# Hybrid attention, selective scan and mixture-of-experts on one core: the sum over the scan's 16 states moves from GpSimd's additions into TensorE's accumulation

## What is computed

```python
def selective_scan(u, delta, A, B, C, D):
    dA = jnp.einsum('bld,dn->bldn', delta, A)
    dB_u = jnp.einsum('bld,bld,bln->bldn', delta, u, B)
    dA_shift = jnp.concatenate([dA[:, 1:], jnp.zeros_like(dA[:, :1])], axis=1)
    dA_cumsum = jnp.exp(jnp.flip(jnp.cumsum(jnp.flip(dA_shift, axis=1), axis=1), axis=1))
    xs = jnp.cumsum(dB_u * dA_cumsum, axis=1) / (dA_cumsum + 1e-12)
    y = jnp.einsum('bldn,bln->bld', xs, C)
    return y + u * D
...
y = selective_scan(x, delta, A, B, C, D)
return jnp.einsum('bld,de->ble', y, W_out) + b_out
```

## Time and profile before

| | us |
|---|---|
| median of 3 runs | 1469.24 (1466.34 to 1470.05) |
| the profiled execution | 1482.02 |
| its span | 1480.3 |
| PE busy | 1006.6 |
| DVE busy | 827.8 |
| ACT busy | 745.5 |
| POOL busy | 633.3 |
| mean granted TensorE clock | 0.788 of 2.4 GHz |

### The profile page before, as it was taken

The page is one execution under the profiler, slowest core; times in us unless marked ns, Lnnn a source line. Parts: engine busy times, 40 slices in busy tenths (PEclk is TensorE's granted clock), DMA queues, the critical chain, the costliest instruction groups (busy, mean ns, idle before and its releaser), DMA issues.

```text
span 1480.3 us, 18066 instructions
## 1 busy us (share of the span) xinstructions
PE 1006.6 (68%) x5080; PEld 742.0 (50%) x5080; DVE 827.8 (56%) x2789; ACT 745.5 (50%) x2034; POOL 633.3 (43%) x672
## 2 busy tenths in 40 slices
PE   4778588757787755588697863678688647871371
PEld 2555377625666433457476622366476316650371
DVE  3677655655565775655566673745656754662111
ACT  4777676646555755545566652352454443450020
POOL 2100400173342537560424268785455686456304
PEclk8565589858797857788888956789889867995696
DMA  9000424222322011334434221254444223523472
GB/s 267 4 1 0 127 93 148 79 85 88 103 88 84 13 33 58 121 96 138 132 105 139 79 81 32 84 160 157 128 150 164 84 63 118 160 83 101 129 220 73
DMA packets 101812, 150.65 MB, mean 102 GB/s; under 512 B 9840, under 2 KB 72688, under 8 KB 101584
## 3 DMA queue, kind: packets, MB, share of 16 engines
q1 hardware_dynamic: 88832, 129.20, 27.9%
q0 software_dynamic: 8528, 18.19, 4.3%
q10 hardware_dynamic: 4352, 2.10, 0.5%
HBM read 125.39 MB, written 28.25 MB: 104 GB/s over the span
## 4 chain that ended last, share of the span: by engine, by line
PE 36%; DVE 20%; ACT 16%; POOL 12%; issue 10%; DMA 4%; another core or an unknown queue 2%; SPq 1%; POOLq 0%; DVEq 0%; ACTq 0%
PE eo_bank L1300 9%; PE h_bank L1285 8%; ACT sc_bank L644 7%; PE sc_bank L1234 6%; DVE Pw L892 4%; POOL xg L564 3%; POOL rings L508 3%; DVE rings L902 3%; DVE nmx L836 3%; PE mix_bank L1157 2%; PE sc_bank L1178 2%; POOL gbuf L577 2%; ACT rings L689 2%; DVE eos L1024 2%
## 5 line engine op out<-in xcount | busy, mean ns | idle before, releaser
L1300 PE MATMUL eo_bank<-wring,hid 128*128 128x128 f32 x1472 | 222.0, 300 | 84.9 <-DVE eos L1024 81.5
L644 ACT ACTIVATE sc_bank<-sc_bank,nmx 128x256 f32<-128x256 f32 x512 | 229.8, 457 | 45.7 <-DVE nmx L836 41.4
L1300 PEld LDWEIGHTS eo_bank<-wring,hid 128*128 128x128 f32 x1472 | 202.5, 213 | 96.2 <-ACT hid L718 51.7
L1285 PE MATMUL h_bank<-xT,wring 128*128 128x128 f32 x1472 | 226.6, 302 | 34.6 <-DVE xT L1012 22.0
L1285 PEld LDWEIGHTS h_bank<-xT,wring 128*128 128x128 f32 x1472 | 204.7, 212 | 70.5 <-issue 33.7
L718 ACT ACTIVATE hid<-h_bank 128x512 f32<-128x512 f32 x184 | 109.2, 594 | 230.2 <-PE h_bank L1285 215.3
L508 POOL TENSOR_TENSOR rings<-Rs,Abc 128x512 f32<-128x512 f32 x128 | 163.0, 1288 | 138.9 <-ACT Rs L672 83.1
L1234 PE MATMUL sc_bank<-Pw,upto 128*128 128x512 f32 x256 | 165.7, 747 | 57.9 <-DVE Pw L892 57.2
L836 DVE TENSOR_REDUCE nmx<-sc_bank 128x2 f32<-128x512 f32 x256 | 169.8, 684 | 58.1 <-PE sc_bank L1178 47.5
L577 POOL DMA_INDIRECT gbuf<-yg,pos x128 | 122.9, 960 | 168.2 <-issue 102.0
L902 DVE SCALAR_TENSOR_TENSOR rings<-sc_bank,bc,rings 128x128 f32<-128x128 f32 x512 | 143.0, 342 | 74.5 <-PE sc_bank L1234 74.2
(11 more groups left out here) (155 smaller groups left out, 1364.5 us busy)
## 6 DMA issues: line engine op xcount, KB each, us to landing
wring<-wcat SPq DMA_DIRECT2D x184, 512.0 KB
stage<-xg SPq DMA_DIRECT2D x40, 256.0 KB, 5.0
yg<-eos SPq DMA_DIRECT2D x40, 256.0 KB
wcat<-in_w SPq DMA_DIRECT2D x16, 256.0 KB, 5.2
X<-in_x SPq DMA_DIRECT2D x16, 128.0 KB, 5.1
xg<-xnb,pos POOLq DMA_INDIRECT x128
gbuf<-yg,pos POOLq DMA_INDIRECT x128
out<-X ACTq DMA_DIRECT2D x16, 128.0 KB
```

The costliest lines, as they stand in the source:

```text
L644: last = act.activation(sc[r % NSC][:, c * L:(c + 1) * L], sc[r % NSC][:, c * L:(c + 1) * L], ACT.Exp, bias=nmx[:, c, r:r + 1], accum_out= ...
L1285: last = pe.matmul(hb[b % 2][:, f], wring[:, n % WR, 0, f], xT[:, b % 2], start=True, stop=True)
L1300: last = pe.matmul(eo[:, o:o + P], hid[:, b % 2, f], wring[:, n % WR, 1, f], start=(k == 0), stop=(k == FC - 1))
```

## The change

The weighted blocks are no longer added by POOL. `scan_yT` now has four parts; a part takes two chunks, that is 8 blocks of 128 x 128, each as the stationary operand of a product with the identity, all accumulating in one region of `mp`. So sum and transpose are one. The skip term is a ninth product in parts 1 and 3. All 8 chunks have a record slot, so ACT's waits for the additions are gone; the first chunk's L waits for the last y of the sequence before. In stages with a head, the parts stand in halves 5 to 8, and all that follows y in them (ACT's copy, projection, norm, logits, routing) stands three halves later (`ST_LATE`); in the others the parts stand in halves 1, 2, 4 and 5 and nothing is shifted.

```diff
-        SLOTS, REC_SLOTS = 4, 6
+        SLOTS, REC_SLOTS = 4, CHUNKS
...
-        ysum = sb("ysum", [P, 4 * D])
-        y_s = sb("y_s", [P, T, P])
...
+        ST_LATE = 3
+        Y_PARTS = {True: (5, 6, 7, 8), False: (1, 2, 4, 5)}
...
-            def scan_sum(b, k):
-
-                c = k // 4
-                pool.wait_ge(*scan_dve.at(f"X{k}", b))
...
-                pool.tensor_tensor(ysum[:], ysum[:], rec_slot(k), ALU.add).then_inc(*scan_pool.done(f"add{k}"))
...
             def scan_rest(b):
 
                 pool.wait_ge(*scan_dve.at("u", b))
-                wait_latest(pool, (scan_pool, "yD", b - 1))
+                wait_latest(pool, (scan_pe, "yT", b - 1))
...
-            def scan_skip(b):
-                pool.wait_ge(*scan_pool.at("y1", b))
-                pool.tensor_tensor(y_s[:], y_s[:], uD[:], ALU.add).then_inc(*scan_pool.done("yD"))
...
             def scan_L(b, k):
 
                 act.wait_ge(*scan_act.at(f"E{k}", b))
-
-                if k >= REC_SLOTS:
-                    last = k - REC_SLOTS
-                    act.wait_ge(*scan_pool.at(f"add{last + (last % 4 == 0)}", b))
-                elif k == 0:
-                    wait_latest(act, (scan_pool, "y1", b - 1))
+                if k == 0:
+                    wait_latest(act, (scan_pe, "yT", b - 1))
...
-            def scan_yT(n, b):
-                if n in head:
-                    pe.wait_ge(*attn_dve.at(f"qk{HG - 1}", head[n]))
-                else:
-                    mp_free(n)
-                pe.wait_ge(*scan_pool.at("yD", b))
-                transposes(mp, y_s, scan_pe, "yT")
+            def scan_yT(n, b, part):
+
+                if part == 0:
+                    if n in head:
+                        pe.wait_ge(*attn_dve.at(f"qk{HG - 1}", head[n]))
+                    else:
+                        mp_free(n)
+                c, k = part // 2, 2 * part + 1
+                pe.wait_ge(*scan_dve.at(f"X{k}", b))
+                y = mp[:, c * P:(c + 1) * P]
+                for i in range(8):
+                    last = pe.matmul(y, rec_slot(k - 1 + i // 4)[:, i % 4 * D:(i % 4 + 1) * D], ident[:],
+                                     start=(part % 2 == 0 and i == 0), stop=False)
+                if part % 2 == 1:
+                    pe.wait_ge(*scan_pool.at("uD", b))
+                    last = pe.matmul(y, uD[:, c], ident[:], start=False, stop=True)
+                if part == 3:
+                    last.then_inc(*scan_pe.done("yT"))
...
-                    if half == 5 and ct is not None:
-                        scan_yT(n, ct)
-                    if half == 6 and ct is not None:
+                    if ct is not None and half in Y_PARTS[a is not None]:
+                        scan_yT(n, ct, Y_PARTS[a is not None].index(half))
+                    if half == 6 + s and ct is not None:
                         scan_proj(ct)
```

More of the change, by code:

```diff
@@ L743, in phase @@
                         attn_oT(at)
-                    if half == 5 and ct is not None:
+                    if half == 5 + s and ct is not None:
                         scan_yT(ct)
@@ L753, in phase @@
                         scan_softplus(c)
-                    if half == 7 and ct is not None:
+                    if half == 7 + s and ct is not None:
                         rstd(prep_act[2], prep_dve[2], ct, p_mv, p_lv, p_rs)
@@ L757, in phase @@
                         rstd(attn_act, attn_dve, head[n + 1], a_mv, a_lv, a_rs)
-                    if half == 8 and ct is not None:
+                    if half == 8 + s and ct is not None:
                         prep_xnT(2, ct)
@@ L763, in phase @@
                         route_exp(1, at // GS)
-                    if half == 11 and ct is not None and ct % GS == GS - 1:
+                    if half == 11 + s and ct is not None and ct % GS == GS - 1:
                         route_exp(2, ct // GS)
@@ L1070, in phase @@
                         route_hot(1, at // GS)
-                    if half == 9 and ct is not None:
+                    if half == 9 + s and ct is not None:
                         prep_top(2, ct)
@@ L1318, in phase @@
                 o = AT_LATE if a is not None else 0
+                s = ST_LATE if a is not None else 0
                 for half in range(HALVES):
```

53 lines of the change are left out of this document (10 added, 43 removed).

## The result

The changed kernel takes **1489.47 us** (median of 4 runs, 1482.32 to 1490.18) where the kernel before takes 1467.95 (4 runs, 1466.34 to 1470.05). The ratio is 1.0135, with an interval of 1.010 to 1.017: slower by 21.5 us. Beside the experiments it was measured again, at 1.0126 (1.0086 to 1.0166).

A forecast was written before the change was run, and what follows sets the result against it. No engine was full; PE bound stages with an expert run, POOL was busiest in 24 and 29. Terms -11.4 - 14.3 + 32.9 + 7.3 + 33.3 = +47.8 us gave 1517 us, own range 1495 to 1545, 8 in 10: 1472 to 1556.

The forecast's parts named there:

- +33.3: Products in stages 25, 26, 27, 28, 30, 31: 6 x 7.3 = +43.8 us, less what covers them, together +33.3.
- The additions' 5.7 us come back in each: -11.4 us: Stages 24 and 29: POOL is 7.9 us late; removing the tail's additions gains 5.7 us in each.
- PE waited for `y_s` 18.9 us in 4 times [...]; no gain is counted: PE's waits for `y_s`: the parts of y take its place, so no gain from 18.9 us.
- The products' price: PE's new products: 0.2225 us each, 7.3 us a sequence, 117 us in all; 73.5 us of products counted in the sum.
- The slope of 0.9 us of time for each us of PE: Stages 10 and 18 against 14 gave 0.88 and 0.95 us of time per us of PE; 0.9 taken.
- The 10.5 us of cover: Token waits in stages 27 and 30 (-3.6), POOL's 4.3 us lateness in 25, run ends in 28 and 31 (-2.6).
- ACT's waits, -14.3 us: ACT's waits for additions before L6: -3.8 us in stage 9, -3.5 in 29, -3 in 24, -2 in 17, -2 all others.
- Rival 1: PE's idle time takes the products in, only POOL's gains stay: 1443.5 us; chance 0.17.
- Rival 2: Denser PE work raises the clock in stages 14, 16, 24 and 29, worth -14 us: 1503; chance 0.08.
- Rival 3: Products of every stage but 24, 29 and 32 lie on the path at 10.0 us: +104, 1573; chance 0.12.
- Rival 4: Half or two thirds of the 73.5 us of products hides: +11 or -1, 1468 to 1480; chance 0.08.
- What would show it: Signs: POOL about 460 us busy, PE about 1140, stages 18 and 27 longer by 6 to 8, 24 and 29 shorter.

The follow-up runs named there:

- kernel 2: The kernel before with eight record slots instead of six, so ACT's L6 and L7 wait for no addition; 1462.48 us, ratio 0.9957.
- kernel 8: The kernel before with eight slots, with PE summing y for sequences 7 and 12 only and POOL for the other fourteen; 1436.51 us, ratio 0.9778.
- kernel 3: The kernel before with only the shift by three halves in stages with a head; 1467.68 us, ratio 1.0.
- kernel 1: The changed kernel without its 32 block products a sequence, only the skip term left in y; 1404.34 us, ratio 0.9569.
- kernel 4: The shifted kernel before, POOL still adding, with 34 more products of constants a sequence at the places of the parts; 1529.11 us, ratio 1.042.
- kernel 10: The version with sequences 7 and 12 on PE, with POOL also adding for them into an unread `y_s`; 1459.66 us, ratio 0.9949.
- kernel 5: The changed kernel with each block product made a second time against zeros, y unchanged; 1593.36 us, ratio 1.0841.
- kernel 9: The version with sequences 7 and 12 on PE, without the block products of these two; 1433.89 us, ratio 0.9777.
- kernel 6: The changed kernel with parts 0 and 1 of y moved behind S7 in stages without a head; 1509.37 us, ratio 1.0279.

## Why the effect was under half of the forecast, and what was right

The effect came out as follows, each step against the one before it: eight slots -7 us (kernel 2); sequences 7 and 12 on PE -26 (kernel 8 against 2); the other fourteen on PE +51 (the changed kernel against 8, 1487.4 to 1436.5). The sum is +18 by these and +21.5 by the first pair of medians.

By place, from the traces (us; stages 31 and 32 go from the `u_s` of stage 31 to the first transpose of the last run). The products' cost is once taken with the additions there (kernel 3 to 4) and once without them (kernel 1 to the changed one), the removal's worth once with the products (kernel 4 to the changed one) and once without (kernel 3 to 1):

| stages | products: forecast | with additions | without | removal: forecast | with products | without |
|---|---|---|---|---|---|---|
| 10 to 22, even | +40.2 | +43.9 | +44.4 | part of -2 | -6.0 | -6.5 |
| 24 and 29 | 0 | +0.1 | 0.0 | -17.9 | -25.8 | -25.7 |
| 25 to 28, 30 to 32 | +33.3 | +23.0 | +43.9 | part of -2, and 4.3 in the +33.3 | -7.2 | -28.1 |

- **The step that failed: "The additions' 5.7 us come back in each: -11.4 us", and with it "PE waited for `y_s` 18.9 us in 4 times [...]; no gain is counted".** What taking the additions away is worth was priced too low, at 25.7 us where it is 40 to 63. In stages 24 and 29 it gave 26 us, not 11.4 (and not 17.9 with ACT's waits). The price was read from R's side: POOL is 7.9 us late, so no more than that can be gained, and 5.7 us is the work that goes. Both bounds were wrong. The 7.9 us was what was left of POOL's lateness *after* R had itself been held 4 to 5 us by PE's wait for `y_s`; with that wait gone it is 12 (kernel 10). And the work that goes is not the tail's share alone: the main share stands in the same list ahead of the scatters, and its waits for X2 and X3 went too. Kernels 8 and 10 show it: 36 to 38 us from exponents to exponents with the additions in the list, 24 to 26 without.
- **The same error in stages 25 to 32, where the larger part of the missing 26 us lies.** The sum gave them +33.3; from kernel 3 to the changed one it is +15.8, which is +43.9 for the products and -28.1 for the removal. The forecast knew 4.3 us of POOL's lateness in stage 25 and none in stage 30, again read behind an R that was itself late in that trace (`uT` to R 14.9 us, for 10.3 to 11.3 in both stages of kernels 2, 3 and 8). Three places of the removal's worth are seen in the traces. They are the 7 and 4 us by which POOL is late in stages 25 and 30 (below), and PE's wait for `y_s` in stage 32, 5.4 us of the 18.9.
- **The products' price was right.** Forecast 73.5 us in all; measured 61 with the additions there and 85 without them (the square above). In stages 25 to 32 it is 43.9 without them, beside the 43.8 from which the forecast took 10.5 for waits. A product took 0.235 us in a dense stretch and 0.25 in the mean, where 0.2225 was taken. The slope of 0.9 us of time for each us of PE is 0.92 for the second set of products (kernel 5: 104 us of time for 113 us of PE), but 0.56 from kernel 3 to 4 (61 for 110). Free in 24 and 29 was right (kernel 9).
- **What covers the products was wrong.** The 10.5 us of cover in stages 25 to 31 (the run's tokens, POOL's lateness in 25, the end of the runs) don't show in the changed kernel. "Nothing behind them can take them in" is wrong where the additions stay: there the products cost 23.0 us. And "two parts stand ahead of S6 and S7 [...], so all lie upstream of R" is wrong for these two in stages 24 and 29: they fill waits of PE there (kernel 6). From the trace before to the changed kernel's the stages with a run and no head grew by 0.3 (stage 25), 0.7 (26), 5.3 (27), 3.9 (28) and 2.9 us (30), which is products less removal.
- **ACT's waits, -14.3 us:** 7 (kernel 2). Stage 9 gave its 3.8; stages 24 and 29 gave 1.2 and 2.1 for 3 and 3.5, with POOL's list as long as before (36.4 and 37.7 us in the table).
- **The shift, 0:** right in sum (kernel 3).
- **Stages with a head and a run, 10, 12, 18, 20, 22:** +3.9, +5.4, +2.3, +4.9 and +12.8 against a forecast of 6.6 each, +29.5 for +32.9 in sum. That 18 has so little and 22 nearly twice its share is in good part the shift's doing: kernel 3 alone has -5.1 and +4.4 there, and the block products by themselves (kernel 1 to the changed one) add 8.8 and 6.7. **Stage 14, half of 7.3:** +3.0.
- **Rival 1** (the products hide): falls by kernels 4 and 5. **Rival 2** (the clock pays): the granted clock of stages 24 and 29 did go from 0.63 to 0.77 and 0.81, and both shrank by far more than 9 us; in stage 29 that is the very sign that the forecast had named. It is not the cause. Kernel 9 has the same short stages at 0.69 and 0.70, and kernel 10 has long ones (62 and 57 us) at a clock of 0.70 as well. The Trainium skill ("TensorE: Matmul & The Clock Gate", the clock gate) says that activity releases the throttle; the trace agrees that the denser stages have the higher clock, but these stages were bound by POOL. The sign was badly chosen, since a POOL that comes free gives it too. **Rival 3:** falls; the groups stood at 0.94 us for four products in the dense stretches, and the time is 84 us below its 1573. **Rival 4** (half or two thirds hidden, 1468 to 1480) is 9.5 us away at its upper end, nearer than the forecast's 1517. Its reason holds only where the additions stay; in the changed kernel the products cost more than forecast, not half.
- **What would show it:** POOL 462 of a forecast 460, ACT's waits gone, first exponents close behind R: right. PE 1100, 94 more for a forecast of 120 to 160; stages 18 and 27 longer by 2.3 and 5.3 (6 to 8 forecast), 24 and 29 shorter by 12.7 and 14.2 (6 to 9 forecast): wrong.

**POOL's lateness in stages 25 and 30.** In kernel 3 R's copy on ACT ends at 956.23 us in stage 25, and POOL's first exponents begin 9.0 us later:

```profile
955.85 0.38 ACT L673 ACTIVATE Rs<-mix_bank 128x256 f32<-128x256 f32 x1
```

```profile
965.28 1.27 POOL L509 TENSOR_TENSOR rings<-Rs,Abc 128x512 f32<-128x512 f32 x1
```

| us | stage 25: `uT` to R | R to first exponents | stage 30: `uT` to R | R to first exponents |
|---|---|---|---|---|
| before | 14.9 | 4.3 | 14.9 | 0.1 |
| kernel 3, additions, no products | 10.7 | 9.0 | 10.3 | 4.0 |
| kernel 4, additions and products | 14.9 | 4.4 | 14.9 | 0.1 |
| kernel 1, neither | 11.0 | 2.0 | 10.3 | 0.1 |
| changed, products alone | 14.0 | 0.1 | 13.9 | 0.1 |

From kernel 3 to 4 the products hold R by 4.2 and 4.6 us, and the first exponents hardly move (from the start of `uT`'s copy 19.7 to 19.3 us, and 14.3 to 15.0), since POOL is late anyway. Without the additions, in stage 30, the same products move them by 3.6 us (kernel 1 to the changed one). So where POOL still adds, part of the products hides in its lateness, which is one reason why they cost 61 us in kernel 4 and 85 in the changed kernel.

What stays open: which waits make up the rest of the 28.1 us in stages 25 to 32, and why the shift alone lengthens stage 22 by 4.4 us. The mean granted clock of that stage is 0.96 in the trace before and 0.84 in kernel 3's (0.84 in the changed kernel's too); that goes with a longer stage, but no run shows it to be the cause.

## What to carry over

Price a removed step on an in-order engine from its list, not from its duration: take the time from the last useful operation ahead of it to the first one behind it, and count the waits that the step brings into the list. When two engines are late at the same point, neither's visible wait is its lateness; work both out from the stage's start. A second trace of the same work with the other engine early (here the shifted kernel's) shows it: 9.0 us where the first showed 4.3. And where an engine is short in some stages and idle in others, move the work only in the latter: two of sixteen sequences gave 26 us here, and the other fourteen together cost 51.

## What the runs showed of the hardware

- On one chip the kernel before took 1457.2 to 1473.5 us over 17 runs, the changed kernel 1482.3 to 1489.5 over 6. One profiled execution of the former held two stalls of 5.6 and 8.0 us, waits of DVE that no engine or queue of the trace ends. A difference of two profiled executions (8.2 us here) can be a third of that of the medians (21.5).
- In stage 24 POOL issues most of its indirect DMAs 1.25 to 1.3 us apart, of which 0.3 is between them ("issue"): the eight gathers of stage 24 take 9.8 us of POOL (901.18 to 910.95), more than the additions' 6.4 us in front of them.
- In stage 22 of the changed kernel eight instructions of an expert block go from 1.06 us to 2.04 us right after a wait of 2.16 us; the granted clock averages 0.56 over the 11 us from 857. Of PE's two levels, 1.2 and 2.4 GHz, that is mostly the lower one:

```profile
851.45 1.06 PE L1261 MATMUL eo_bank<-wring,hid 128*128 128x128 f32 x8
...
856.96 2.04 PE L1261 MATMUL eo_bank<-wring,hid 128*128 128x128 f32 x8 [2.16 <-DVE eos L973]
```

```profile
857.00:868.00 11.00, 10.57 (x50) 9.13 (x50) 4.11 (x14) 5.71 (x23) 0.00 (x0) 0.56 0.09 25
```
